# The third layer's cross-attention in a four-layer kernel: narrow queries, block-diagonal keys, and softmax sums inverted on GpSimd

## The reference

```python
B, LQ, D = 4, 256, 256;  LK = 64;  H = 16;  HD = 16
x = layer_norm(hidden, ln1_w, ln1_b)
q = (x @ q_w + q_b).reshape(B, LQ, H, HD).transpose(0, 2, 1, 3)
k = (ctx @ k_w + k_b).reshape(B, LK, H, HD).transpose(0, 2, 1, 3)
v = (ctx @ v_w + v_b).reshape(B, LK, H, HD).transpose(0, 2, 1, 3)
scores = jnp.einsum('bhqd,bhkd->bhqk', q, k) / sqrt(HD)
scores = jnp.where(mask, scores, finfo.min)
attn = softmax(scores, axis=-1)
out = jnp.einsum('bhqk,bhkd->bhqd', attn, v).transpose(0, 2, 1, 3).reshape(B, LQ, D)
hidden = out @ cproj_w + cproj_b + hidden
return hidden + (gelu(layer_norm(hidden, ln2_w, ln2_b) @ fc_w + fc_b) @ proj_w + proj_b)
```

## Time and profile before

| | us |
|---|---|
| median of 3 runs (942.02 to 944.42) | 943.88 |
| the profiled execution, its own time | 942.92 |
| its span in the trace | 941.1 |
| busy in the span: PE / VectorE / ScalarE / GpSimd | 864.7 / 615.5 / 486.8 / 483.4 |
| L2's projection begins on PE | 516.0 |
| first scores of L2 | 536.2 |
| last row addition of L2's attention ends | 597.9 |

### The profile page before, as it was taken

The page is one execution under the profiler, slowest core; times in us unless marked ns, Lnnn a source line. Parts: engine busy times, 40 slices in busy tenths (PEclk is TensorE's granted clock), DMA queues, the critical chain, the costliest instruction groups (busy, mean ns, idle before and its releaser), DMA issues.

```text
span 941.1 us, 16083 instructions
## 1 busy us (share of the span) xinstructions
PE 864.7 (92%) x5808; PEld 719.8 (76%) x5808; DVE 615.5 (65%) x1344; ACT 486.8 (52%) x1189; POOL 483.4 (51%) x508
## 2 busy tenths in 40 slices
PE   4788876899999999999899898999999999999898
PEld 3677755899976689767788686899966689766798
DVE  3788887426779767798442499417779757798340
ACT  2566655654753346632662344755753357533562
POOL 2767876474544245465385054464543345464383
PEclk8799999999999999999999999999999999999999
DMA  6833212002460014300000200202450024100001
GB/s 191 295 97 97 95 39 69 34 2 68 157 236 1 1 45 159 134 0 1 1 24 5 86 2 1 102 1 86 162 213 1 1 67 158 46 0 1 1 13 34
DMA packets 26674, 64.06 MB, mean 68 GB/s; under 512 B 2995, under 2 KB 15843, under 8 KB 25444
## 3 DMA queue, kind: packets, MB, share of 16 engines
q1 hardware_dynamic: 26596, 63.03, 20.2%
HBM read 57.22 MB, written 5.77 MB: 67 GB/s over the span
## 4 chain that ended last, share of the span: by engine, by line
PE 68%; DVE 20%; issue 5%; POOL 4%; ACT 1%; DMA 1%; SPq 1%; DVEq 0%; POOLq 0%
PE ps L960 7%; PE ps L900 6%; PE ps L859 6%; PE ps L861 6%; PE ps L889 5%; PE ps L936 4%; PE ps L758 3%; PE ps L701 3%; PE ps L702 3%; PE ps L703 3%; PE ps L682 3%; DVE prob L1640 3%; PE ps L683 3%; PE ps L684 3%; DVE mx L1639 3%
## 5 line engine op out<-in xcount | busy, mean ns | idle before, releaser
L960 PE MATMUL ps<-arena,pT_all 128*128 128x256 f32 x512 | 116.9, 382 | 5.8 <-DVE x L1660 3.7
L960 PEld LDWEIGHTS ps<-arena,pT_all 128*128 128x128 f32 x512 | 96.6, 191 | 32.3 <-issue 15.2
L936 PE MATMUL ps<-arena,hT 128*128 128x512 f32 x256 | 115.5, 594 | 0.0
L543 POOL TENSOR_TENSOR arena<-arena,rinv 128x640 f32<-128x640 f32 x64 | 80.3, 1256 | 53.4 <-DVE rinv L1454 53.3
L570 POOL TENSOR_TENSOR prob<-prob,rinv 128x512 f32<-128x512 f32 x32 | 49.5, 1547 | 113.3 <-DVE rinv L1653 113.3
L536 POOL TENSOR_TENSOR rstd<-var,neg_half 128x1 f32<-128x1 f32 (+1 forms) x56 | 33.9, 605 | 139.8 <-DVE var L1469 139.8
L1189 ACT ACTIVATE arena<-ps,nb 128x320 f32<-128x320 f32 x128 | 66.3, 523 | 56.7 <-DVE nb L1440 56.6
L1225 ACT ACTIVATE arena_r<-ps,cols 128x256 fp32r<-128x256 f32 x128 | 66.5, 520 | 54.2 <-PE ps L684 54.2
L512 POOL TENSOR_TENSOR vacc<-vacc,vpart 128x256 f32<-128x256 f32 x60 | 43.9, 732 | 98.6 <-ACT vpart L1297 98.4
L589 POOL TENSOR_TENSOR arena_r<-arena,arena_r 128x512 fp32r<-128x512 f32 x64 | 83.9, 1330 | 14.6 <-ACT arena L1226 14.6
L682 PE MATMUL ps<-hH,w1H 128*128 128x256 f32 x256 | 74.8, 292 | 11.9 <-DVE prob L1640 5.1
(11 more groups left out here) (166 smaller groups left out, 2325.2 us busy)
## 6 DMA issues: line engine op xcount, KB each, us to landing
ring<-in_heads_dram SPq DMA_DIRECT2D x64, 512.5 KB, 3.3
w<-in_w_dram SPq DMA_DIRECT2D x8, 1024.0 KB, 7.4
first_r<-spare_k SPq DMA_DIRECT2D x24, 160.0 KB
first_q<-spare_q SPq DMA_DIRECT2D x48, 64.0 KB, 2.4
spare_k<-HL SPq DMA_DIRECT2D x8, 320.0 KB, 2.4
spare_q<-HL SPq DMA_DIRECT2D x8, 256.0 KB, 2.5
x<-in_x_dram SPq DMA_DIRECT2D x1, 1024.0 KB, 6.0
lnb<-in_lnb_dram SPq DMA_DIRECT2D x4, 256.0 KB, 6.8
```

What stands on the lines that cost most here:

```text
L543: g.tensor_tensor(w, w, rinv[:, n % 2, 0:2].unsqueeze(2).broadcast_to([P, 2, KEYS0]), ALU.mult)\
L936: last = mm(ps[:, SCORES[k][half], :], hT[:, k, d, 0:P], A[:, d, b // 2, cols_of, sl, :].rearrange("p r s k -> p r (s k)"), start=(d == 0) ...
L960: last = mm(ps[:, 6, 0:D], pT[:, k, c, :], VW[:, b, c, :], start=(c == 0), stop=(c == PAIRS - 1))
```

## The change

Queries and keys of L2 are no longer padded: `wp2` holds 256 columns of each. `queries` makes 4 products for 8, into the second half of bank 0. The keys are block-diagonal: a strip of 32 rows holds two heads, and each of the two `kc` jobs is copied out twice, with a column of ones and zeros (`L2_parity`) as scale, so that one head's rows are kept and the other's are zero; the clear at L594 shrinks to 1024 columns. `scores` runs on four strips of 32 rows, into the first halves of banks 0 to 3, after four products of one row each (`ones_r` times `mask2`) that write the mask. VectorE's maximum and subtraction are done in two halves; the first raises `s2_half`, for which the next `queries` waits.

The softmax's sums go another way: ScalarE copies them from PSUM (`sum2`), GpSimd raises them to the power -1 (`inv2`), and VectorE multiplies a round later. `values` and `output` move one round later (i-2 and i-3), `values` ahead of `queries` on PE; the row additions too, and the loop has 11 rounds. Weight splits come in twos from GpSimd's round 2 on. The first tile's transposes stand ahead of `project`, the first queries behind it, and only the last of 6 jobs waits for the rows of the layer before.

The core of the diff:

```diff
@@ gpsimd
-            for n in range(TILES):
+            for n in range(TILES + 2):
                 if n + 2 < TILES:
                     power("L2", n + 2, 1)
-                pool.wait_ge(z_ready, 2 * TILES + n + 1)
-                add_row(x, n, "L2_cproj_b")
-                if n >= 4:
-                    for j in range(4 * n - 16, 4 * n - 12):
-                        split_weights(2, j)
-            power("M2", 0, 2)
-            power("M2", 1, 2)
+                if n < TILES:
+                    pool.wait_ge(z_ready, 2 * TILES + n + 1)
+                    add_row(x, n, "L2_cproj_b")
+                if n >= 2:
+                    pool.wait_ge(sum2_ready, n - 1)
+                    if n >= 4:
+                        pool.wait_ge(oT_ready, n - 3)
+                    g.tensor_tensor(inv2[:, n % 2, :], sum2[:, n % 2, :], neg_one[:, 0:1].broadcast_to([P, D]), ALU.pow)\
+                        .then_inc(inv2_ready, 1)
+                    split_weights(2, 2 * n - 4)
+                    split_weights(2, 2 * n - 3)
+                if n in (TILES - 2, TILES - 1):
+                    power("M2", n - (TILES - 2), 2)
@@ tensor
                     if g >= 1:
-                        pe.wait_ge(q_ready, g)
-                    for m in range(4):
+                        pe.wait_ge(s2_half, g)
+                    for m in range(DH):
...
-                    for m in range(4):
-                        for s in range(2):
-                            at = slice(C * s, C * s + C)
-                            last = mm(ps[:, s, m * P:(m + 1) * P], qT2[at, k, m, :], KC[at, m, b, :], start=True, stop=True)
+                    for j in range(4):
+                        at = slice(32 * j, 32 * j + 1)
+                        mm(ps[:, j, 0:D], ones_r[at, :], mask2[at, b * C:(b + 1) * C].unsqueeze(1).broadcast_to([1, 4, C]),
+                           start=True, stop=False)
+                    for m in range(DH):
+                        for j in range(4):
+                            at = slice(32 * j, 32 * j + 32)
+                            last = mm(ps[:, j, m * P:(m + 1) * P], qT2[at, k, m, :], KC[at, m, b, :],
+                                      start=False, stop=(m == 1))
...
                 turn_z2(0)
+                pe.wait_ge(in_l2, 48)
+                project()
+                pe.wait_ge(proj_act, 1)
+                queries(0)
                 turn_z2(1)
-                queries(0)
-                for i in range(TILES + 2):
+                pe.wait_ge(proj_act, NJ // 2)
+                pe.wait_ge(proj_dve, NJ // 2)
+                for i in range(TILES + 3):
                     if i < TILES:
                         scores(i)
                     if 1 <= i <= TILES:
                         turn_p(i - 1)
-                    if i + 1 < TILES:
-                        queries(i + 1)
-                    if 2 <= i <= TILES:
-                        output(i - 2)
                     if i + 2 < TILES:
                         turn_z2(i + 2)
...
+                    if 2 <= i <= TILES + 1:
+                        values(i - 2)
+                    if i + 1 < TILES:
+                        queries(i + 1)
...
+                    if i >= 3:
+                        output(i - 3)
@@ scalar
+                    if i >= 2:
+                        act.wait_ge(pv_ps, i - 1)
+                        if i >= 4:
+                            act.wait_ge(inv2_ready, i - 3)
+                        a_(sum2[:, i % 2, :], ps[:, 4, D:2 * D], ACT.Copy).then_inc(sum2_ready, 1)
@@ vector
                     dve.wait_ge(pv_ps, g + 1)
-                    link(v.reciprocal(inv2, ps[:, 2, D:2 * D]))
-                    v.tensor_tensor(oT[:, g % 2, :, :], ps[:, 2, 0:D].rearrange("p (d n) -> p d n", d=DH),
-                                    inv2.rearrange("p (d n) -> p d n", d=DH), ALU.mult).then_inc(oT_ready, 1)
+                    dve.wait_ge(inv2_ready, g + 1)
+                    v.tensor_tensor(oT[:, g % 2, :, :], ps[:, 4, 0:D].rearrange("p (d n) -> p d n", d=DH),
+                                    inv2[:, g % 2, :].rearrange("p (d n) -> p d n", d=DH), ALU.mult).then_inc(oT_ready, 1)
...
-                for i in range(TILES + 2):
-                    if i >= 2:
-                        values(i - 2)
+                for i in range(TILES + 3):
                     if i < TILES:
                         k = i % 2
                         dve.wait_ge(s_ps, base + i + 1)
...
+                        for half in range(2):
+                            two = slice(2 * half, 2 * half + 2)
+                            main = ps[:, two, 0:D].rearrange("p j (m c) -> p j m c", c=C)
...
+                            link(v.tensor_reduce(mj, main, AX.X, ALU.max))
+                            v.tensor_tensor(pm, main, mj.unsqueeze(3).broadcast_to([P, 2, 4, C]), ALU.subtract)\
+                                .then_inc(s2_half if half == 0 else s_used, 1)
...
+                    if i >= 3:
+                        values(i - 3)
```

More of the change, by code:

```diff
@@ L333, in up_slot @@
             if b == 0 and l > 0:
-                bank, half = (((0, 4, 5, 6) if l == 2 else (0, 1, 2, 5))[f // 2], f % 2)
+                bank, half = ((0, 1, 2, 5)[f // 2], f % 2)
             else:
@@ L344, in turn_bank @@
             return TURN_M[l][b] if b < 2 else 4
-        JOBS = [("kc", m) for m in range(4)] + [("vc", b) for b in range(B)]
+        JOBS = [("kc", m) for m in range(DH)] + [("vc", b) for b in range(B)]
         NJ = len(JOBS)
@@ L1039, in values @@
                         pe.wait_ge(oT_ready, g)
-                    for s in range(2):
+                    for m in range(DH):
                         for w in range(2):
-                            for m in range(4):
-                                c = 4 * s + m
-                                at = slice(32 * m, 32 * m + 32)
-                                what = VC[:, b, c, :, :].rearrange("p e c -> p (e c)") if w == 0 else sums_of[:, :]
-                                last = mm(ps[at, 2, w * D + s * P:w * D + (s + 1) * P], what, pT[:, k, c, :],
+                            for j in range(4):
+                                at = slice(32 * j, 32 * j + 32)
+                                what = VC[:, b, 4 * m + j, :, :].rearrange("p e c -> p (e c)") if w == 0 else sums_of[:, :]
+                                last = mm(ps[at, 4, w * D + m * P:w * D + (m + 1) * P], what, pT[:, k, 2 * j + m, :],
                                           start=True, stop=True)
@@ L1053, in output @@
                         pe.wait_ge(rows_done, rows_before("L2") + g)
+                    if g < 4:
+                        pe.wait_ge(h_ready, base + g + 6 if g < 3 else base + TILES)
+                    else:
+                        pe.wait_ge(s_used, base + TILES)
                     for d in range(DH):
-                        last = mm(ps[:, 3, 0:D], oT[:, g % 2, d, :], vw2[:, 1, d, :], start=(d == 0), stop=(d == 1))
+                        last = mm(out2(g), oT[:, g % 2, d, :], vw2[:, 1, d, :], start=(d == 0), stop=(d == 1))
                     last.then_inc(o_ps, 1)
@@ L1146, in _, with copy @@
             a_ = nc.scalar.activation
-            def copy(out, in_, bias):
+            def copy(out, in_, scale, bias):
                 if bias is None:
                     return a_(out, in_, ACT.Copy)
-                return a_(out, in_, ACT.Identity, bias=bias)
+                return a_(out, in_, ACT.Identity, scale=scale, bias=bias)
             act.wait_ge(pool_set, 1)
@@ L1352, in attend2 @@
                     job_out(act, copy, n).then_inc(proj_act, 1)
-                scaled(base, "L2_ln1_w", "L2_ln1_b")
                 scaled(base + 1, "L2_ln1_w", "L2_ln1_b")
-                for i in range(TILES + 1):
-                    if i >= 1:
+                for i in range(TILES + 2):
+                    if 1 <= i <= TILES:
                         n, k = base + i - 1, (i - 1) % 2
@@ L1401, in link, with copy @@
                 dve.wait_ge(dve_step, steps[0])
-            def copy(out, in_, bias):
+            def copy(out, in_, scale, bias):
                 if bias is None:
                     return v.tensor_copy(out, in_)
-                return v.tensor_scalar(out, in_, bias, None, ALU.add)
+                return v.tensor_scalar(out, in_, scale, bias, ALU.mult, ALU.add)
             v.memset(Q0[0:96, :, :, :, :].bitcast(F32), 0.0).then_inc(q0_set, 1)
@@ L1768, in _halves, with _of_parity @@
     return np.ascontiguousarray(np.asarray(w).reshape(-1, P, w.shape[-1]).transpose(1, 0, 2))
-def _padded(w):
-    out = np.zeros((w.shape[0], H, 32), w.dtype)
-    out[:, :, :HD] = w.reshape(w.shape[0], H, HD)
-    return out.reshape(w.shape[0], H * 32)
-def _padded_bias(v, row16):
-    out = np.zeros((H, 32), v.dtype)
-    out[:, :HD] = v.reshape(H, HD)
-    out[:, HD] = row16
-    return out.reshape(4, P).T
-def _by_strip(v):
```

(6 more changed lines are left out.)

122 lines of the change are left out of this document (60 added, 62 removed).

## The result

The changed kernel takes 1270.29 us (median of four runs, 1270.03 to 1274.05), the kernel before, run on the same chip in turn with it, 944.15 (four runs, 942.02 to 945.03). The ratio is 1.3463, with a 95% interval from 1.3441 to 1.3484: slower by a third. The forecast was 1235, the range ended at 1255. The direction and the mechanism were right, and the time lies 35 us above the forecast and 15 above the range.

The account below looks back on a forecast made before the run. VectorE was taken to set the round, PE close behind. First inversion at 540.3, plus 294.4 for eight, 43.7 of gaps, then multiply, output, addition: 880.4 against 597.9, +282.5; clock +9; on 942.9 that gave 1235 us, range 945 to 1255.

Parts of the forecast that it names:

- Projection: Ahead of the L2 attention: eight jobs become six and the first scores start at 526.1 against 536.19, 10.1 us gained.
- Inversion: GpSimd raises 128x256 softmax sums to the power -1, eight times, not hidden: 36.8 us each, 0.564 + 255 x 0.142.
- the step of 0.04: Smaller price per further column of GpSimd's power, 0.706 - 0.67 = 0.04 us, putting one inversion at 9.7 us.
- Order and gaps: L2 loop: inversions can't overlap; splits, root, normalise, softmax, multiply, values and copy lie between them, seven gaps summing to 43.7 us.
- Clock: PE, idle during inversions, returns at lower clock: 0.9 in each of seven gaps, some 3 at MLP's start, +9 us.
- One stall of some 5.5 us: Token loop before the change, 557.5 to 569.5: GpSimd splits weights in fours and the chain runs through it, 12.0 against 6.5.
- second rival: Power at the addition's price, 0.8 us; lock-step of PE and VectorE bounds L2: 944, between 935 and 955; chance 0.12.
- Third rival: Power as cheap, L2 rounds at their busy time, 6.0 us, because PE's values don't wait: 930; chance 0.10.
- The tail: From the last L2 softmax to the last row addition: 13.8 us now and one step more, 16, for the 930 case.
- Fourth rival: L2 scores on PE: strips run in series, narrow layout doesn't pay; at most 10 us on top of any case.

## Why the prediction was right and wrong, point by point

**Projection: right.** The first mask products of the scores start at 528.05 in the profile after, and the row addition ahead of L2 at 517.89, against 536.19 and 515.25 before: 20.9 us became 10.2, a gain of 10.8 where 10.1 was forecast. That the row addition itself came 2.6 us later is not the change's doing: in the profiles of the two other kernels that are the kernel before up to this point (the series of widths, the weight splits in twos) it starts at 516.09 and 517.18, and in those of the changed kernels anywhere from 514.98 to 518.76. So positions of two profiles are compared here from that row addition on.

**Inversion: right mechanism, the term mis-sized.** This is the step that missed the range: "36.8" for one inversion, from 0.564 + 255 x 0.142. It is 41.14. Eight times the difference are 34.7 us, and the time is 35.3 above the forecast. The step of 0.142 was taken between the first and the second column; from the fourth column on it is 0.156 to 0.160, and 0.159 where the rows are long. The range's own note, "a step of 0.13 to 0.145 a column", came from nothing but that pair of rows. Its upper end is worth 8 x 255 x 0.003 = 6 us, not the 25 that the note gives, and the measured step lies 12% above 0.142. Even a tenth to either side, 29 us, would have ended at 1264; a slope from two neighbouring short rows, carried 255 columns out, bore no range as narrow as that. The lower bounds (0.76 us by the addition's rows, 9.7 by the step of 0.04) were both far off.

The Trainium skill's GPSIMD Engine Reference, section 3.1, by which the prediction had 0.8 us, is near what a product takes (0.61 us at 128x256), as it was for the addition (0.756). It accounts for an add, not for a power, which costs 67 times a product of that shape.

**Order and gaps: right.** From the starts of the eight inversions (541.42, 591.38, 641.34, 691.36, 735.64, 787.55, 835.66, 879.91), less 41.15 each, the gaps are 8.8, 8.8, 8.9, 3.1, 10.8, 7.0 and 3.1: 50.5 us. The forecast was 43.7 and 0.9 for the clock in each, 50.0. The first began 1.1 later than forecast, the 2.6 of above less 1.5 won.

**Clock: right in the gaps, too high behind them.** Of the 9 us, 6.3 stood in the gaps and are there. From the last row addition's end to the span's end are 344.2 us in the profile after and 343.2 before, so the MLP's cold start cost 1 us, not 3. On the other side, the steps from the last inversion's end to the last row addition's took 3.1 us for 2.0, with PE's output at 2.09 us for 1.13. With the 34.7 of the inversions, 0.5 of the gaps and 1.1 of the first start, and the 2 less at the MLP's start, that is the 35.

**No stall where one was read.** "One stall of some 5.5 us" compared a stretch of 12 us with one round, when it held two. It cost the sum nothing, since nothing was credited for it, but the second rival claimed it as won. A look at successive softmaxes of the tile loop would have told it: 6.5 and 5.8 us apart.

**Second rival, at its own condition: too low.** With the power at a product's price it gives 944; the kernel that meets this condition takes 953.5, at the upper edge of the rival's 935 to 955. The mechanism, PE and VectorE in series, is what the traces show. The missing term is in the main the clock: the prediction counted it behind waits of 36 us, and left it out behind waits of 2 to 4 us. By the rows of the profile with the product, pieces at the lower level cost 1.6 to 1.7 us in three rounds and 0.9 in a fourth, and the first two rounds, behind the fall at 530, took 5.7 and 4.8 us for the 4.1 of the kernel after: about 8 us. From the row addition ahead of L2 to the last one in it the profile has 7.0 us more than before, where the rival had 0.5. This is worked out from rows, not tried by itself; a wait of 2.8 us for GpSimd's root, at 546.41, is another part that the rival left out.

**Third rival: its round was seen once, its time never.** It gave 930 if a power were cheap and PE's values didn't wait behind the softmax. The kernel with the product and the multiplication ahead of the softmax meets both, and took 947.7. Its one round without a wait for the root took 5.8 us, near the 6.0 of the rival; the others, 8.3 to 10.3, waited 1.4 to 3.4 us for it. The prediction had this path through GpSimd's queue for the inversion, and left it out of the rival. With VectorE's own reciprocal the rounds were 7.1, 6.5 and 7.5 us and the time 943. The tail, put at "one step more", was the other part: outputs behind the MLP's products.

**Fourth rival: false.** Mask products and scores start 0.22 us apart, and the sixteen score products take 0.62 us (550.50 in the kernel with VectorE's reciprocal) for the 1.19 of 64-row strips before, near the lower bound of 0.55. For the same number of products that is half the time, as of twice as many strips at once.

## What to carry to other kernels

Before an operation moves to an idle engine, find its own row there at two widths far apart; a neighbour operation of the same shape says nothing about it, and an idle engine is no cover when the result is needed in the same round. A power on GpSimd is priced by the column, so it belongs where few columns remain (16 columns took 2.9 us here, 256 took 41).

When PE and VectorE hand work to each other, put what the other engine waits for ahead of your own long instructions: moving the reciprocal and the multiplication ahead of the softmax was worth some 20 us, more than the 14 us of the eight reciprocals themselves. Price waits of PE of a few us twice, once as idle time and once in the products that may follow at the lower clock.

## What the runs showed of the hardware

The power in GpSimd's two-operand instruction costs 0.156 to 0.160 us for each further column of 128 partitions from the fourth on (41.1 us for 256, 81.9 for 512). Exponents -1 and -1/2, and sources of 5.3, of ones and of squares, gave the same to 0.01 us.

The granted clock falls behind waits of a few us within a loop, too. With PE waiting 3.9 and 4.4 us in a round it was 0.50 to 0.59 in the 4 us behind each; with waits of 1.1 to 2.4 us (the kernel with the output ahead of `up`) it was 1.00 from 546 to 570. It isn't a matter of the waits alone: in the run with the product it had fallen to 0.51 at 530 to 534, behind an idle time of 1.3 us, at a place where the kernel after, with the same instructions, kept 1.00. What decides there stays open.
